# First expert slot's columns from a permutation product, and context keys taken from the chip, in a two-layer gated cross-attention kernel

## What is computed

```
x = x + tanh(g_xattn[0]) * cross_attention_0(layernorm(x), ctx)
x = x + tanh(g_ffn[0])   * experts_0(layernorm(x))
x = x + tanh(g_xattn[1]) * cross_attention_1(layernorm(x), ctx)
x = x + tanh(g_ffn[1])   * (self attention, then 16 experts)(layernorm(x))
```

```
route = sigmoid(t @ router_w)                 # 1024 rows, 8 experts
e     = argmax(route)                         # one expert for each row
out   = (silu(t @ gate_w[e]) * (t @ up_w[e])) @ down_w[e] * max(route)
k_img = rms_norm(ctx @ k_img_w.T + k_b) * norm_k   # keys of stage three, 8 batches of context
v_img = ctx @ v_img_w.T + v_b
```

## Time and profile before

| | us |
|---|---|
| median of three runs | 778.97 |
| lowest and highest of them | 778.62, 780.02 |
| profiled execution, its time | 778.13 |
| its span in the trace | 776.4 |
| first product of slot 0 (from the span's start) | 112.00 |
| end of the last slot's down product | about 200.4 |

### The profile page before, as it was taken

How to read it: one execution, slowest core, us unless ns; L and a number is a source line. 1 busy time by engine, 2 the same in 40 slices (tenths; PEclk the granted TensorE clock), 3 DMA queues, 4 the chain that set the end, 5 groups by cost and what they waited for, 6 DMA issues and landing times.

```text
span 776.4 us, 13496 instructions
## 1 busy us (share of the span) xinstructions
PE 742.0 (96%) x4636; PEld 605.4 (78%) x4637; DVE 421.1 (54%) x806; ACT 342.9 (44%) x813; POOL 248.7 (32%) x298
## 2 busy tenths in 40 slices
PE   8999989999869989999999999999989999999998
PEld 6787746666557767889988998898868888888886
DVE  6878451121467774544454445445564565656565
ACT  3888212222258773544454445444453332233223
POOL 5203240000444673732222321322223443444430
PEclk9999999999989999999999999999999999999999
DMA  8970221111300010101101100010014334333331
GB/s 315 420 278 2 55 81 35 47 41 41 109 15 2 1 35 1 35 22 55 35 20 34 54 20 34 20 62 21 0 41 126 97 119 115 115 114 102 115 101 55
DMA packets 25606, 58.04 MB, mean 75 GB/s; under 512 B 3536, under 2 KB 14416, under 8 KB 24288
## 3 DMA queue, kind: packets, MB, share of 16 engines
q1 hardware_dynamic: 24800, 55.42, 21.9%
q0 software_dynamic: 768, 2.10, 0.8%
HBM read 51.41 MB, written 6.09 MB: 74 GB/s over the span
## 4 chain that ended last, share of the span: by engine, by line
PE 80%; DVE 7%; ACT 6%; POOL 3%; DMA 2%; issue 2%; SPq 0%; DVEq 0%; POOLq 0%; ACTq 0%
PE PS L338 15%; PE PS L340 15%; PE PS L339 15%; PE PS L1636 7%; PE PS L1378 7%; PE PS L1393 3%; PE PS L445 3%; PE PS L478 2%; PE PS L487 2%; PE PS L451 2%; PE PS L1642 2%; PE PS L500 1%; POOL Z L816 1%; DVE x_mx L834 1%; PE PS L433 1%
## 5 line engine op out<-in xcount | busy, mean ns | idle before, releaser
L338 PE MATMUL PS<-tTh,wh 128*128 128x512 f32 x200 | 78.4, 392 | 1.4 <-ACT act_s L1170 0.9
L1181 ACT ACTIVATE hhh<-hh 128x512 fp32r<-128x512 f32 x50 | 31.6, 632 | 105.1 <-DVE hh L1207 94.7
L340 PE MATMUL PS<-tTh,wl 128*128 128x512 f32 x200 | 77.9, 390 | 0.0
L339 PE MATMUL PS<-tTl,wh 128*128 128x512 f32 x200 | 77.9, 389 | 0.0
L637 DVE TENSOR_TENSOR hhl<-hh,hhh 128x512 fp32r<-128x512 f32 x50 | 52.4, 1048 | 34.9 <-ACT hhh L1181 34.9
L1747 ACT ACTIVATE sm<-sm,nmx 128x128 f32<-128x128 f32 x128 | 49.6, 389 | 37.7 <-DVE nmx L1810 37.7
L1273 POOL CAST wh<-wraw 128x512 fp32r<-128x512 f32 (+1 forms) x50 | 26.1, 523 | 110.6 <-PE PS L340 110.6
L637 DVE TENSOR_TENSOR oTl<-PS,oTh 128x512 fp32r<-128x512 f32 x32 | 22.1, 691 | 71.6 <-ACT oTh L1741 71.6
L1275 POOL TENSOR_TENSOR wl<-wraw,wh 128x512 fp32r<-128x512 f32 (+1 forms) x50 | 58.0, 1160 | 8.4 <-POOL wh L1273 7.9
L1850 POOL CAST ah<-araw 128x512 fp32r<-128x512 f32 (+1 forms) x32 | 16.2, 506 | 134.4 <-PE PS L340 134.4
L1378 PE MATMUL PS<-WE,xsT 128*128 x120 | 56.4, 594 | 0.1
(11 more groups left out here) (255 smaller groups left out, 1844.0 us busy)
## 6 DMA issues: line engine op xcount, KB each, us to landing
WE<-moe SPq DMA_DIRECT2D x8, 1536.0 KB, 14.3
wraw<-moe SPq DMA_DIRECT2D x25, 384.0 KB, 3.0
araw<-attn SPq DMA_DIRECT2D x16, 384.0 KB
cwb<-cw_d SPq DMA_DIRECT2D x20, 256.0 KB, 3.9
WX<-wx SPq DMA_DIRECT2D x2, 1024.0 KB, 8.3
avraw<-attn_v SPq DMA_DIRECT2D x8, 256.0 KB
xs_d<-zeros SPq DMA_DIRECT2D x1, 1920.0 KB, 17.7
xs_s<-xs_d SPq DMA_DIRECT2D x15, 128.0 KB, 2.0
```

The costliest lines, as they stand in the source:

```text
L338: nc.tensor.matmul(out, wh_, xh_, start=first, stop=False, **kw)
L339: nc.tensor.matmul(out, wh_, xl_, start=False, stop=False, **kw)
L340: return nc.tensor.matmul(out, wl_, xh_, start=False, stop=last, **kw)
L1181: nc.scalar.activation(hhh[half][:, :], hh[half][:, :], ACT.Copy).then_inc(s.hi_done, 1)
```

## The change

1. **Slot 0's columns without the scatter.** TensorE first multiplies `earlier` by `ones`, which gives in bank 6, in every partition, the numbers 0 to 127. VectorE compares them with `posf` in one operation of 128x1024 and so writes `perm`: for each batch a 128x128 matrix with a one where a row's position is that of the column. `perm` lies in the memory of the two `gs` buffers. TensorE then multiplies the rows of all eight batches by it, 16 matmuls of 128 columns, and has the columns of slot 0 in bank 5, from where ScalarE copies them as before. All rows are still scattered; slot 0 isn't loaded back, and the first loads are of slots 1 and 2.
2. **Keys in another order.** `KEYS` is 4, 5, 6, 7, 0, 1, 2, 3. The first four take the context from `cT`. Only batches 0 to 3 are loaded over `rT`, and TensorE waits for them at the fifth. The banks of the first six are 1, 7 and 3 in turn.
3. **Places.** The first key product stands ahead of the place products, with 2 fills in place of 8; the second and third behind them, in place of 7 fills; the fourth behind the permutation product; the fifth and sixth inside slot 0. There the up product follows the gate product at once, and `turn_hidden(0)` and `down(0, 0)` are done in slot 0, before the columns of slot 1. The 10 and 2 fills are gone.
4. **VectorE.** Three small operations (`scaled_bq`, `bo1`, the ones of `V1`) move ahead of the routing chain. The comparison stands between `pos` and the table of experts. The first four key batches follow that table, the other two stand in slot 0 behind `hs`; `normalise_keys` follows the output rows of slot 0.

```diff
+KEYS = [*range(B - CTX, B), *range(B - CTX)]
...
+        gs2 = sb("gs", [P, 2, I0], where=e)
+        perm = gs2[:, :, :].rearrange("p a n -> p (a n)").rearrange("p (b s) -> p b s", b=B)
@@ ffn_pe
-            fill(8, 0)
+            def keys_values(i):
+                b = KEYS[i]
+                after(pe, s.kv_free, 2 * i - 4 if i < MOST else 0)
+                for c in range(C):
+                    src = xb0.cT[b % CTX][:, c, :] if i < CTX else rT[:, c, b * S:(b + 1) * S]
+                    m = nc.tensor.matmul(kv_bank(i), src, WX[1][:, c, 0:2 * D], start=(c == 0), stop=(c == C - 1))
+                m.then_inc(s.kv_done, 1)
+            nc.tensor.matmul(PS[:, 6, 0:P], ones[:, :], earlier[:, :], start=True, stop=True).then_inc(s.ids_done, 1)
+            pe.wait_ge(wx_in[1], 16)
+            keys_values(0)
+            fill(2, 0)
...
-            fill(7, 0)
-            pe.wait_ge(s.ctx_in, 16 * C)
-            pe.wait_ge(wx_in[1], 16)
-            for b in range(MOST):
-                after(pe, s.kv_free, 2 * b - 6)
-                keys_values(b)
+            keys_values(1)
+            pe.wait_ge(s.place_read, 1)
+            keys_values(2)
+            pe.wait_ge(s.perm_done, 1)
+            for c in range(C):
+                for b in range(B):
+                    m = nc.tensor.matmul(PS[:, 5, c * P:(c + 1) * P], FX[:, b, c * P:(c + 1) * P], perm[:, b, :], start=(b == 0), stop=(b == B - 1))
+            m.then_inc(s.xt_done, 1)
+            keys_values(3)
...
-                if not is_first(j):
+                if is_first(j):
+                    up(e, par, 1, s.u_done)
+                    pe.wait_ge(s.ctx_in, 16 * C)
+                    keys_values(4)
+                    turn_hidden(0)
+                    keys_values(5)
+                    down(0, 0)
+                    pe.wait_ge(s.kv_free, 2 * MOST)
+                    columns(1, 1)
+                    return
+                if not is_second(j):
                     turn_hidden(j - 1)
...
-            fill(10, 0)
-            columns(0, 1)
-            fill(2, 0)
             slots(pe, tile)
@@ ffn_dve
             v.tensor_copy(pos[:, :], posf[:, :]).then_inc(s.pos_done, 1)
+            dve.wait_ge(s.ids_done, 1)
+            v.tensor_tensor(perm, PS[:, 6, 0:P].unsqueeze(1).broadcast_to([P, B, P]), posf[:, :].unsqueeze(2).broadcast_to([P, B, P]), ALU.is_equal).then_inc(s.perm_done, 1)
...
-                if not is_first(j):
+                if is_first(j):
+                    keys_values(4, MOST)
+                    output_rows(0, 0, 0)
+                    normalise_keys(dve, 0, MOST, 1)
+                elif not is_second(j):
                     output_rows(j - 1, 1 - par, i + 1)
@@ ffn_sp
+            rest = B - CTX
             for c in range(C):
-                sp.dma_start(rT[:, c, :].rearrange("p (b s) -> p b s", b=B), ctx_d[:, :, c, :].rearrange("b p s -> p b s")).then_inc(s.ctx_in, 16)
+                sp.dma_start(rT[:, c, 0:rest * S].rearrange("p (b s) -> p b s", b=rest), ctx_d[0:rest, :, c, :].rearrange("b p s -> p b s")).then_inc(s.ctx_in, 16)
             sp.wait_ge(s.scattered, 16 * B)
-            load(0, 0)
             load(1, 1)
+            load(2, 0)
```

More of the change, by code:

```diff
@@ L147, in build @@
         xsT = [sb(f"xsT{i}", [P, C, P], where=e) for i in range(2)]
-        gs = [sb(f"gs{i}", [P, I0], where=e) for i in range(2)]
+        gs2 = sb("gs", [P, 2, I0], where=e)
+        gs = [gs2[:, i, :] for i in range(2)]
+        perm = gs2[:, :, :].rearrange("p a n -> p (a n)").rearrange("p (b s) -> p b s", b=B)
         hs = sb("hs", [P, I0], where=e)
@@ L1338, in is_first, with is_second @@
             return isinstance(j, int) and j == 0
+        def is_second(j):
+            return isinstance(j, int) and j == 1
         def tile_rows(d, j):
@@ L1416, in ffn_pe, with key_columns @@
             down(SLOTS - 1, (SLOTS - 1) % 2)
[L1418 to L1422, removed]
+            for i in range(MOST, B):
+                keys_values(i)
+            for i in range(B):
+                if i == MOST:
                     pe.wait_ge(s.kt_free, 3)
                     fill(15, 2)
-                pe.wait_ge(s.k1_ready, 1 if b < MOST else 2)
-                after(pe, s.kt_free, b - 3)
+                pe.wait_ge(s.k1_ready, 1 if i < MOST else 2)
+                after(pe, s.kt_free, i - 3)
                 for c in range(C):
-                    m = nc.tensor.transpose(PS[:, b % 4, c * P:(c + 1) * P], K1[:, b, c * P:(c + 1) * P], ident[:, :])
+                    m = nc.tensor.transpose(PS[:, i % 4, c * P:(c + 1) * P], K1[:, KEYS[i], c * P:(c + 1) * P], ident[:, :])
                 m.then_inc(s.kt_done, 1)
[L1431 to L1435, removed]
+        def key_columns(act, i0, i1):
+            for i in range(i0, i1):
+                act.wait_ge(Es.kt_done, i + 1)
+                nc.scalar.activation(K1[:, KEYS[i], :], PS[:, i % 4, 0:D], ACT.Copy).then_inc(Es.kt_free, 1)
         def ffn_act(act):
@@ L1461, in ffn_act, with kv_bank, normalise_keys @@
             key_columns(act, 0, MOST)
[L1463 to L1466 removed]
+        def kv_bank(i):
+            return PS[:, (1, 7, 3)[i % 3] if i < MOST else 4 + i - MOST, :]
+        def normalise_keys(dve, i0, i1, group):
             dve.wait_ge(Es.krs_done, group)
[L1469 to L1471 removed]
+            for i in range(i0, i1):
+                b = KEYS[i]
+                m = nc.vector.scalar_tensor_tensor(out=K1[:, b, :], in0=K1[:, b, :], scalar=krs8[:, i:i + 1], in1=vec("nk1"), op0=ALU.mult, op1=ALU.mult)
+            m.then_inc(Es.k1_ready, 1)
         def add_experts(dve, ch, b):
@@ L1505, in ffn_dve @@
             dve.wait_ge(s.place_done, 1)
-            ch.link(v.tensor_copy(place[:, :, :].rearrange("p b e -> p (b e)"), PS[:, 3, 0:(B + 1) * E0]))
+            v.tensor_copy(place[:, :, :].rearrange("p b e -> p (b e)"), PS[:, 3, 0:(B + 1) * E0]).then_inc(s.place_read, 1)
+            dve.wait_ge(s.place_read, 1)
             ch.link(v.tensor_tensor(more_than[:, :, :], place[:, B, :].unsqueeze(2).broadcast_to([P, E0, B]),
@@ L1524, in ffn_dve, with keys_values @@
             v.tensor_copy(ex[:, :], exf[:, :]).then_inc(s.experts_done, 1)
[L1526 to L1531, removed]
-                                    vec("bv1").rearrange("p (h d) -> p h d", d=XD), ALU.add).then_inc(s.kv_free, 1)
[L1533 to L1544, removed]
+            def keys_values(i0, i1, done=True):
+                for i in range(i0, i1):
+                    b = KEYS[i]
+                    dve.wait_ge(s.kv_done, i + 1)
+                    v.tensor_tensor(K1[:, b, :], kv_bank(i)[:, 0:D], vec("bk1"), ALU.add).then_inc(s.kv_free, 1)
+                    v.tensor_tensor(V1[:, b, :, 0:XD], kv_bank(i)[:, D:2 * D].rearrange("p (h d) -> p h d", d=XD),
+                                    vec("bv1").rearrange("p (h d) -> p h d", d=XD), ALU.add).then_inc(s.kv_free, 1)
+                    dve.wait_ge(s.kv_free, 2 * i + 1)
+                    m = mean_square(K1[:, b, :], kjunk[:, :], kms8[:, i:i + 1])
+                    if i < i1 - 1 or not done:
+                        ch.link(m)
+                if done:
+                    m.then_inc(s.kms_done, 1)
             def output_rows(j, par, stores):
@@ L1597, in tile @@
             def tile(j, par, i):
-                if not (isinstance(j, int) and j + 2 >= SLOTS):
+                if not is_first(j) and not (isinstance(j, int) and j + 2 >= SLOTS):
                     sp.wait_ge(s.xt_done, j + 1)
```

24 lines of the change are left out of this document (13 added, 11 removed).

## The result

Median 775.36 us (773.39 to 777.58, five runs), beside 779.42 (778.62 to 780.02, five runs) of the kernel before: ratio 0.9949, 95% interval 0.9927 to 0.9970. That is 4.1 us faster; forecast was 3.4 us and 775.6. Two more series of the changed kernel, on other occasions, gave 775.36 (eleven runs) and 775.18 (six runs).

A forecast was written before the change was run, and what follows sets the result against it. TensorE's chain, left for 15 us through scatter and load before slot 0, bounds it. Slot 0 7.6 us earlier, less 3.44 (keys) and 0.78 (pause), gives 3.4 us: 778.97 to 775.6; range 773.8 to 777.5.

The forecast's parts named there:

- Front, +0.83: TensorE's list ahead of the place products, partly at half clock: the place result reaches VectorE 0.83 us later.
- (a): Rival at the front: clock stays up or falls later, no delay of the place result; gain 4.2 us, 774.8; chance 0.12.
- (b): Rival: slow stretch over the whole front, delay 2.3 us in place of 0.83; gain 1.9, 777.1; chance 0.12.
- Moved VectorE operations, 0: Three operations ahead of the routing chain, 0.68 us, fit into 0.85 us of VectorE idle time: cost nothing, 0.17 to spare.
- Comparison, 1.22: VectorE's comparison writing `perm`, priced at 1.224 us from an operation of the same shape; TensorE loses 0.2 us there.
- Product, 4.4: TensorE's permutation product ahead of slot 0, 32 records: 4.4 us, from a row of 8 records in 1.10 us.
- Slot 0 to slot 2, +4.22: From slot 0's to slot 2's first product: 9.74 us before, plus two key batches (3.44) and a pause (0.78).
- Slack of slot 1's load, 1.6: Slot 1's rows land at 111.8, TensorE comes to them at 113.4: 1.6 us of slack.
- Normalising: VectorE's normalising of keys ends at 116.8, `hs` of slot 1 is wanted at 118.1: slack 1.3 us.
- (c) A later slow stretch moves.: Rival: a half-clock stretch near 217.0 or 288.7 is lost or gained, 1.25 to 1.7 us either way; chance 0.10.
- (d): Rival: half clock goes on over keys, comparison and product, costing up to 7.2 us, 782.8, slower than before; chance 0.04.

The follow-up runs named there:

- a_fill3: The changed kernel with 21 fills instead of 10 ahead of stage three: 774.81 us, ratio 0.9937 to the kernel before.
- a_double: The changed kernel with the permutation product done twice over, the second pass overwriting the first with the same numbers: 783.99 us, ratio 1.0061 to the kernel before.

## Why the prediction was right, point by point

The direction, the mechanism and the place held: the chain left the scatter, and slot 2 came earlier. That the median is within 0.3 us of the forecast 775.6 is partly luck: the gain was 0.7 us larger than forecast, the median of the kernel before came out 0.45 us higher with two more executions (779.42 for 778.97), and in the profiled execution two deviations worked against each other, as told below. Measured from the last router product, slot 2's gate came at 28.0 instead of 32.4, 4.4 us earlier instead of 3.4. The terms:

- **Front, +0.83.** The place copy came at 5.29 instead of 4.71: +0.58. The sum had the half clock from 90.7 to 94.1; it was granted from 90.0 to 93.4, and so ended ahead of the place products. The other runs measured the bounds: -0.26 at full clock and +1.95 with 6.8 us at half clock, against 0 and 2.3 in the text (all from before's 4.71). Rivals (a) and (b) are thus no other theories but other executions of the same front. The Trainium skill ("TensorE: Matmul & The Clock Gate", What's actually happening) has the count of slow matmuls of one kernel vary from run to run at its start; here the same was seen 90 us into it, with 0, 3.4 and 6.8 us at half clock.
- **Moved VectorE operations, 0.** 0.16 us of idle time was left, 0.17 forecast.
- **Comparison, 1.22.** It took 1.22. The pause of TensorE ahead of the product, forecast 0.2, was 0.05.
- **Product, 4.4.** 3.84, and 3.67 from its start to that of the next product. This is the term that was most mis-sized, by 0.6 to 0.7 us: the row with 8 records in 1.10 (137 ns each) carries its start and end in a short group, while 32 in a row took 115 ns each from start to start. Of the two estimates from the Trainium skill, four passes ("FP8 and Floating Point Precision", TensorE Precision Notes) at 134 cycles each ("TensorE: Matmul & The Clock Gate", Back-to-back issue gap), 3.6 us, was nearer; the one from that section's 81 ns for each pair, 5.2 us, was not borne out.
- **Slot 0 to slot 2, +4.22.** 13.7 us in the chain of waits (103.43 to 117.16) instead of 9.74: +4.0. The two batches were the forecast 3.44 us; the pause ahead of slot 1 was 0.55 (112.70 to 113.25) where 0.78 was forecast.
- **Slack of slot 1's load, 1.6.** SyncE issued it at 109.49, and the loads in this stretch landed 2.0 us later, at 111.5; TensorE came at 112.3. 0.8 us, less than forecast because TensorE was a us earlier. A further gain of that size between the place copy and slot 1 would make the load the bound again; a gain ahead of the place copy moves the scatter too (in a_fill3 the load is issued at 108.63 and TensorE comes at 111.6).
- **Normalising.** Done at 115.9, `hs` of slot 1 at 117.2: 1.3 us of slack, as forecast.
- **(c) A later slow stretch moves.** It did, in the profiled execution: 3.4 us more at 223.1. Shown by the clock rows; that the change caused it isn't shown.
- **(d)** The clock came back at 93.4 in the profile, with the fills gone, and no trace had half clock during the product. It didn't come about in any of them.

In the profiled execution the 1.1 us gained beyond the sum and the 1.7 us of the later stretch partly cancelled, so that its span fell by 2.8 us. The median's 4.1 us lies between that and the 4.4 us of the slots.

## What to carry to other kernels

When a wait for a transfer is replaced by computing the same thing, count what else stands between the new producer and its consumer: here the product without the freed key work, and the freed key work without the product, each gave nothing that could be told from noise. Replacing filler by real work on a stretch whose clock may be at half makes the time depend on the clock: here one batch of keys made the place copy 0.5 to 1.2 us later than fills did at a similar clock. Price a stream from a row of similar length, since a short group carries its start and end.

## What the runs showed that I had not expected

The changed kernel's front ran at full clock, at half clock for 3.4 us or for 6.8 us in different executions of the same code. With fills ahead of stage three the mean clock rose from 0.989 to 0.993, but the time gained was less than 2 us. The first weight transfer landed 2.5 us apart in two executions and moved everything behind it. And 64 product records in a row (a_double) were followed by signals that reached ScalarE and VectorE 2 to 4 us late, costing 2.7 us at slot 0 beyond the work, which the same length of fills didn't.
